# A 16-batch channel-attention block on one core: reordered loads and set-up, split products for one combined weight, and a last row stored in pieces

## What is computed

```python
g_x     = conv1x1(g_w, g_b, ctx)              # CI x N
theta_x = conv1x1(theta_w, theta_b, x)        # CI x N
phi_x   = conv1x1(phi_w, phi_b, ctx)          # CI x N
W = einsum('bnc,bcm->bnm', theta_x.T, phi_x) / N
y = einsum('bnm,bmc->bnc', W, g_x.T).T
wy = conv1x1(w_w, w_b, y)
out = bn_gamma * (wy - bn_mean) * rsqrt(bn_var + eps) + bn_beta + x
```

## Time and profile before

| | us |
|---|---|
| median of 3 runs (lowest and highest) | 789.48 (789.16 to 789.52) |
| the profiled execution, by the same clock | 790.07 |
| its span, first to last instruction | 788.3 |
| PE busy in the span | 772.0 (98%) |
| PE weight loads busy | 666.7 |
| DVE, ACT, POOL busy | 498.1, 303.7, 527.5 |

### The profile page before, as it was taken

The page is one execution under the profiler, slowest core; times in us unless marked ns, Lnnn a source line. Parts: engine busy times, 40 slices in busy tenths (PEclk is TensorE's granted clock), DMA queues, the critical chain, the costliest instruction groups (busy, mean ns, idle before and its releaser), DMA issues.

```text
span 788.3 us, 11592 instructions
## 1 busy us (share of the span) xinstructions
PE 772.0 (98%) x4045; PEld 666.7 (85%) x4045; DVE 498.1 (63%) x889; ACT 303.7 (39%) x514; POOL 527.5 (67%) x358
## 2 busy tenths in 40 slices
PE   4999999999999999999999999999999999999997
PEld 4688888888888888888888888888888888888886
DVE  3796574847657496574847657496574847657254
ACT  3634542325334243542325334243542325334131
POOL 4969785767857578585767857578585767857400
PEclk9999999999999999999999999999999999999999
DMA  9828254181733707255181733707255181730202
GB/s 237 197 108 214 107 129 192 35 226 62 178 142 74 246 0 213 106 124 195 33 228 58 178 142 72 247 0 213 106 121 198 32 228 60 178 143 1 107 1 106
DMA packets 55127, 103.17 MB, mean 131 GB/s; under 512 B 2474, under 2 KB 37956, under 8 KB 55108
## 3 DMA queue, kind: packets, MB, share of 16 engines
q1 hardware_dynamic: 52976, 101.86, 44.2%
q10 hardware_dynamic: 2132, 1.05, 0.8%
HBM read 69.35 MB, written 33.55 MB: 131 GB/s over the span
## 4 chain that ended last, share of the span: by engine, by line
PE 96%; DVE 1%; DMA 1%; ACT 1%; issue 0%; DVEq 0%; SPq 0%
PE wbank L667 57%; PE gbank L667 37%; PE wbank L830 1%; DMA ctx_sb<-in_ctx_dram 1%; PE wbank L708 1%; DVE x_sb L486 0%; PE wbank L686 0%; PE wbank L714 0%; ACT x_sb L366 0%; DVE tmp L509 0%; DVE tmp L508 0%; ACT x_hi L340 0%; DVE junk L590 0%; DVE x_sb L657 0%; DVE th_lo L583 0%
## 5 line engine op out<-in xcount | busy, mean ns | idle before, releaser
L286 POOL TENSOR_TENSOR ctxT_lo<-ctxT,ctxT_hi 128x512 fp32r<-128x512 f32 x124 | 167.2, 1349 | 205.7 <-ACT ctxT_hi L340 205.7
L297 POOL TENSOR_TENSOR ctx_sum<-ctx_sum,ctxT 128x512 f32<-128x512 f32 x108 | 157.0, 1454 | 0.2
L315 POOL TENSOR_TENSOR x_lo<-x_sb,x_hi 128x1024 fp32r<-128x1024 f32 x60 | 142.3, 2403 | 0.0
L340 ACT ACTIVATE mt<-wbank 128x512 fp32r<-128x512 f32 x64 | 37.9, 597 | 236.6 <-PE wbank L667 236.6
L657 DVE SCALAR_TENSOR_TENSOR x_sb<-wbank,const,x_sb 128x512 f32<-128x512 f32 x112 | 78.9, 747 | 73.1 <-PE wbank L667 73.1
L667 PE MATMUL wbank<-ctxT_lo,ctxT_hi 128*128 128x512 f32 x512 | 121.6, 393 | 0.0
L518 DVE TENSOR_TENSOR stage<-gbank,mt 128x384 f32<-128x384 f32 x64 | 28.3, 486 | 139.7 <-PE gbank L667 139.7
L667 PEld LDWEIGHTS wbank<-ctxT_lo,ctxT_hi 128*128 128x128 f32 x512 | 95.5, 190 | 18.7 <-POOL ctxT_lo L286 0.2
L340 ACT ACTIVATE ctxT_hi<-ctxT 128x512 fp32r<-128x512 f32 x124 | 76.5, 628 | 88.1 <-DVE ctxT L486 88.1
L667 PE MATMUL gbank<-ctxT_hi 128*128 128x384 f32 (+1 forms) x512 | 80.8, 314 | 10.1 <-ACT ctxT_hi L340 10.1
L667 PEld LDWEIGHTS gbank<-ctxT_hi 128*128 128x128 f32 x512 | 80.0, 191 | 12.0 <-issue 10.1
(11 more groups left out here) (107 smaller groups left out, 1327.4 us busy)
## 6 DMA issues: line engine op xcount, KB each, us to landing
x_sb<-in_x_dram SPq DMA_DIRECT2D x16, 2048.0 KB, 7.8
out_dram<-x_sb SPq DMA_DIRECT2D x64, 512.0 KB, 2.6
ctx_sb<-in_ctx_dram SPq DMA_DIRECT2D x60, 512.0 KB, 8.4
ctx_sb<-in_ctx_dram ACTq DMA_DIRECT2D x4, 256.0 KB, 7.1
ctx_sb<-in_ctx_dram SPq DMA_DIRECT2D x4, 256.0 KB, 7.2
x_sb<-in_L_xattn_w_w_dram SPq DMA_DIRECT2D x1, 512.0 KB, 11.7
stage<-in_L_xattn_theta_w_dram SPq DMA_DIRECT2D x1, 512.0 KB, 12.5
phi_nat<-in_L_xattn_phi_w_dram SPq DMA_DIRECT2D x1, 512.0 KB, 12.7
```

The source lines that it names most:

```text
L286: nc.gpsimd.tensor_tensor(ctxT_lo[:, c, :], turned_ctx(b, c), f(ctxT_hi[:, c, :]), ALU.subtract).then_inc(sem_, 1)
L297: nc.gpsimd.tensor_tensor(ctx_sum[:, :], ctx_sum[:, :], src, ALU.add).then_inc(ctxT_used, 1)
L315: nc.gpsimd.tensor_tensor(x_lo[:, k, :], x_sb[par][:, k, :], f(x_hi[:, k, :]), ALU.subtract).then_inc(x_lo_made, 1)
L340: nc.scalar.activation(dst, src, ACT.Copy).then_inc(sem_, 1)
```

## The change

What it does, in five parts:

1. **Loads.** `bn_var` and `bn_gamma` are loaded first, one on SP's and one on ACT's queue, into `norm_rows`. SP then loads the partition groups 0 and 1 of the first context and ACT the groups 2 and 3 (before: 0 and 2, 1 and 3), both halves ahead of the other vectors on SP. `g_w` comes right behind `w_w`, then x, then `theta_w` and `phi_w` (before: w, theta, phi, x, g).
2. **Scale.** A PE instruction of its own (`turn_norm`) turns these two vectors ahead of all else, and DVE computes the scale before its first `transpose_chunk`. The other vectors are turned behind Gram chunk 4.
3. **Z and ZB.** ACT and DVE make hi and lo parts of g_w (`g_hi`, `g_lo`), of the wide g_b (`bg_hi`, `bg_lo`) and of the turned w (`wsT_hi`, `wsT_lo`; they lie in `th_hi`, `th_lo`, `q_hi` and `q_lo`). Each fp32 matmul of `make_z` becomes three fp32r matmuls.
4. **Other work in batch 0.** `x_lo` of k = 1 moves from POOL to DVE. `next_ctx()` moves on DVE from ahead of `theta(0)` to behind the computation of `const`, and `next_hi(0)` to `next_hi(3)` move on ACT behind the parts of `t_hi`.
5. **Last row.** In the last batch, row m = 3 is made in three pieces (512, 256 and 256 positions) one after the other, each added up and stored by itself.

```diff
         first_half = x_sb[1][:, 2:4, :].rearrange("p a (b c) -> p (a b) c", b=2)
+
...
 
         FIRST_M_BANK = [wbank[4], wbank[1], wbank[2], wbank[0]]
         W_BANK = [wbank[3], wbank[4]]
+        NORM_BANK = VEC_BANK = wbank[3]
         TP_BANK = [wbank[1], wbank[2], wbank[0], wbank[3]]
...
-            load_first_ctx(sp, (0, 2), 0)
-            load_vectors(sp, range(0, 4))
-            load_first_ctx(sp, (0, 2), 1)
+            sp.dma_start(norm_rows[KC:2 * KC, :], bn_var.rearrange("(m p) -> m p", p=P)).then_inc(in_norm, 16)
+            load_first_ctx(sp, (0, 1), 0)
+            load_first_ctx(sp, (0, 1), 1)
+            load_vectors(sp, range(0, 3))
             sp.dma_start(w_nat, w_w.rearrange("(m p) c -> p m c", p=P)).then_inc(in_w1, 16)
+            sp.dma_start(g_nat, g_w.rearrange("(k p) c -> p k c", p=P)).then_inc(in_w2, 16)
+            load_x(0, 0)
             sp.dma_start(theta_nat, theta_w.rearrange("(k p) c -> p k c", p=P)).then_inc(in_w4, 16)
             sp.dma_start(phi_nat[:, :, :], phi_w.rearrange("(k p) c -> p k c", p=P)).then_inc(in_w3, 16)
-            load_x(0, 0)
-            sp.dma_start(g_nat, g_w.rearrange("(k p) c -> p k c", p=P)).then_inc(in_w2, 16)
             sp.dma_start(bp_row[:, :], phi_b.partition_broadcast(P)).then_inc(in_bp, 16)
...
-                for m in range(KC):
+                for m in range(KC if nxt else KC - 1):
                     sp.wait_ge(work_free, NO * b + NH * (m + 1))
                     sp.dma_start(out[b].rearrange("(m p) n -> m p n", p=P)[m], x_sb[par][:, m, :]).then_inc(stored, 16)
+                if not nxt:
+                    m = KC - 1
+                    for i, (a, n, bank) in enumerate(LAST_PIECES):
+                        sp.wait_ge(work_free, NO * b + (NH * m + i + 1))
+                        sp.dma_start(out[b].rearrange("(m p) n -> p m n", p=P)[:, m, a:a + n],
+                                     x_sb[par][:, m, a:a + n]).then_inc(stored, 16)
...
-            for k in range(1, KC):
+            for k in (2, 3):
...
-            load_first_ctx(act, (1, 3), 0)
-            load_vectors(act, range(4, 8))
-            load_first_ctx(act, (1, 3), 1)
+            act.dma_start(norm_rows[0:KC, :], bn_gamma.rearrange("(m p) -> m p", p=P)).then_inc(in_norm, 16)
+            load_first_ctx(act, (2, 3), 0)
             act.wait_ge(ident_done, 2)
             nc.scalar.activation(tmp[:, 7, :], ident[:, 0:KC], ACT.Sqrt)
+            load_first_ctx(act, (2, 3), 1)
+            act.wait_ge(vec_step, 1)
+            nc.scalar.activation(tmp[:, 1, :], tmp[:, 0, :], ACT.Sqrt).then_inc(root_done, 1)
+            load_vectors(act, range(3, 6))
...
+            act.wait_ge(vec_taken, 1)
             for k in range(KI):
                 nc.scalar.activation(bg_wide[:, k, :], f(ones_r[:, :]), ACT.Identity,
                                      scale=bg_col[:, k:k + 1]).then_inc(wide_made, 1)
+            act.wait_ge(in_w2, 16)
+            hi(g_hi, g_nat, g_hi_made)
+            act.wait_ge(wide_made, KI)
+            hi(bg_hi, bg_wide, bg_hi_made)
...
+                if i > 1:
+                    act.wait_ge(w_turned, i - 1)
+                    hi(wsT_hi[:, i - 2, :], W_BANK[i - 2][:, :], w_hi_made)
...
-                if first(b):
-                    next_hi(0)
-                    next_hi(1)
-                    next_hi(2)
...
-                next_hi(3)
+                if not first(b):
+                    next_hi(3)
...
                 if first(b):
-                    next_hi(4)
-                    next_hi(5)
+                    for c in range(6):
+                        next_hi(c)
...
-            dve.wait_ge(in_first[0], 16 * QT)
-            for c in range(RING):
...
+            dve.wait_ge(norm_turned, 1)
             chain(nc.vector.tensor_scalar(ve, var_, EPS, None, ALU.add))
-            dve.wait_ge(in_first[1], 16 * QT)
-            transpose_chunk(0, 4)
             dve.wait_ge(root_done, 1)
             chain(nc.vector.reciprocal(r0, root))
...
             chain(nc.vector.tensor_tensor(r0, r2, gamma_, ALU.mult))
             nc.vector.tensor_scalar(scale[:, :], r0, 1.0 / N, None, ALU.mult).then_inc(scale_made, 1)
+            for h in range(2):
+                dve.wait_ge(in_first[h], 16 * QT)
+                for c in range(RING):
+                    transpose_chunk(0, h * RING + c)
+            dve.wait_ge(vec_turned, 1)
+            nc.vector.tensor_copy(vec_cols[:, :], VEC_BANK[:, 0:3 * KC + 3 * KI]).then_inc(vec_taken, 1)
...
+            dve.wait_ge(g_hi_made, 1)
+            nc.vector.tensor_tensor(g_lo, g_nat, f(g_hi), ALU.subtract).then_inc(g_lo_made, 1)
+            dve.wait_ge(bg_hi_made, 1)
+            nc.vector.tensor_tensor(bg_lo, bg_wide, f(bg_hi), ALU.subtract).then_inc(bg_lo_made, 1)
             first_x_lo_part(0)
-            dve.wait_ge(w_turned, KI)
+            first_x_lo_part(1)
             for k in range(KI):
-                nc.vector.tensor_copy(wsT[:, k, :], W_BANK[k][:, :]).then_inc(w_taken, 1)
+                dve.wait_ge(w_hi_made, k + 1)
+                nc.vector.tensor_tensor(wsT_lo[:, k, :], W_BANK[k][:, :], f(wsT_hi[:, k, :]),
+                                        ALU.subtract).then_inc(w_taken, 1)
...
                 if first(b):
-                    next_ctx()
                     dve.wait_ge(in_bp, 16)
...
                 if first(b):
+                    dve.wait_ge(vec_taken, 1)
                     chain(nc.vector.tensor_tensor(wm, wb_, mean_, ALU.subtract))
                     chain(nc.vector.tensor_tensor(r3, wm, r0, ALU.mult))
                     chain(nc.vector.tensor_tensor(const[:, :], r3, beta_, ALU.add))
+                    next_ctx()
                     transpose_chunk(b + 1, 4)
                     transpose_chunk(b + 1, 5)
                 if nxt:
...
+                pe.wait_ge(ident_done, 2)
+                pe.wait_ge(in_norm, 16 * 2)
+                nc.tensor.transpose(NORM_BANK[:, 0:2 * KC], norm_rows, ident[0:2 * KC, 0:2 * KC]).then_inc(norm_turned, 1)
+
             def turn_vectors():
-                pe.wait_ge(ident_done, 2)
...
             def make_z():
-                pe.wait_ge(in_w2, 16)
+                pe.wait_ge(g_lo_made, 1)
                 pe.wait_ge(w_taken, 2)
                 for j in range(KC):
                     pe.wait_ge(tp_taken, (1, 2, 2, 3)[j])
+                    cols = slice(j * P, (j + 1) * P)
                     for k in range(KI):
-                        ins = nc.tensor.matmul(Z_BANK[j][:, :], g_nat[:, k, j * P:(j + 1) * P], wsT[:, k, :],
-                                               start=k == 0, stop=k == KI - 1)
+                        mm(Z_BANK[j][:, :], g_hi[:, k, cols], wsT_hi[:, k, :], k == 0, False)
+                        mm(Z_BANK[j][:, :], g_hi[:, k, cols], wsT_lo[:, k, :], False, False)
+                        ins = mm(Z_BANK[j][:, :], g_lo[:, k, cols], wsT_hi[:, k, :], False, k == KI - 1)
                     ins.then_inc(z_done, 1)
                 pe.wait_ge(tp_taken, 4)
-                pe.wait_ge(wide_made, KI)
+                pe.wait_ge(bg_lo_made, 1)
                 for k in range(KI):
-                    ins = nc.tensor.matmul(ZB_BANK[:, :], bg_wide[:, k, :], wsT[:, k, :], start=k == 0,
-                                           stop=k == KI - 1)
+                    mm(ZB_BANK[:, :], bg_hi[:, k, :], wsT_hi[:, k, :], k == 0, False)
+                    mm(ZB_BANK[:, :], bg_hi[:, k, :], wsT_lo[:, k, :], False, False)
+                    ins = mm(ZB_BANK[:, :], bg_lo[:, k, :], wsT_hi[:, k, :], False, k == KI - 1)
                 ins.then_inc(zb_done, 1)
...
-                        if c == 1:
+                        if c == RING:
                             turn_vectors()
...
+                def last_row(m):
+                    for a, n, bank in LAST_PIECES:
+                        if bank is OUT_BANK[1][0]:
+                            pe.wait_ge(work_free, NO * b + (NH + 1))
+                        for k in range(KI):
+                            q_h, q_l = q_hi[:, k, m * P:(m + 1) * P], q_lo[:, k, m * P:(m + 1) * P]
+                            mm(bank[:, 0:n], q_h, th_hi[:, k, a:a + n], k == 0, False)
+                            mm(bank[:, 0:n], q_h, th_lo[:, k, a:a + n], False, False)
+                            ins = mm(bank[:, 0:n], q_l, th_hi[:, k, a:a + n], False, k == KI - 1)
+                        ins.then_inc(out_done, 1)
```

66 lines of the change are left out of this document (40 added, 26 removed).

## The result

The changed kernel takes 795.20 us in the median of 6 executions (794.80 to 795.86), the kernel before 789.62 on the same chip (789.16 to 790.80). The ratio is 1.0067, 95% interval 1.0056 to 1.0078: slower by two thirds of a per cent. The profiled execution took 795.54 with a span of 793.8, which is 5.5 more than the span before, and its mean granted clock (TensorE's clock as a share of 2.4 GHz) is 0.995. Two executions, 859.13 us of the kernel before and 1105.55 us of the warm-start experiment, ran at mean clocks of 0.853 and 0.656 and are left out of the ratios and ranges here.

What follows compares the result with a forecast made beforehand. PE was taken as the bound (96% of the chain), with no slack to make up batch 0 delays. Stall +4.3, clock +2.4 and end -1.7 gave +5.0 on the median 789.48: 794.5 us, range 791.5 to 797.5.

Steps and rivals of the forecast that it cites:

- stall and loss of clock: Main case: PE stalls before batch 0's output rows, then runs at a lowered clock; 794.5 us, chance 0.70.
- Part 1, loads and scale: Program start: PE starts at 10.56 us, scale chain off the path, PE's 1.09 wait before w's second half gone.
- The step that the small load ahead delays the context by 0.43: Program start: a small load's issue on the queue moves PE's start from 10.13 to 10.56 us.
- Part 2, Z and ZB: Batch 0: thirty fp32r matmuls save 1.83, but Z may start later; ZB ends 0.9 earlier.
- E: End of ZB in batch 0: predicted 38.5 us, against 39.40 before.
- Part 3, the stall: Batch 0: eight turns, held by POOL through the ring, delay Q's bias term; PE stalls 6.1, output rows +4.3 us.
- Part 4, the clock: Batch 0 output rows: PE's clock falls during the stall and costs 2.4 us, between 0 and 3.1.
- Part 5, the end: Last row: shorter last DVE instruction and smaller last store give 1.7 us, bounds 0.85 to 1.9.
- Sum: Whole kernel: +4.3 + 2.4 - 1.7 = +5.0 us.
- no loss of clock: Rival: the same stall before batch 0's output rows, but full clock after; 792.1 us, chance 0.10.
- the ring that doesn't hold DVE: Rival: batch 0's eight turns pass without waiting for POOL, no stall; 786.0 us, chance 0.08.
- The worse front: Rival: late first loads or theta and phi add 1 to 3 us to the stall; 796.5 us, chance 0.12.

Runs made afterwards that it cites:

- warm-start experiment: plain Z kernel plus 15 thrown-away fp32 identity matmuls on PE while it waits for the first context; 784.56 us, ratio 0.9934.
- plain Z: Q-first kernel with Z and ZB as ten plain fp32 matmuls, without hi and lo parts of g, its bias and w; 784.80 us, ratio 0.9943.
- old-place experiment: Changed kernel with batch 1's first four context turns and their hi parts back ahead of theta(0); 788.58 us, ratio 0.9982.
- the move alone: Kernel before, with only the four turns moved behind const and their hi parts behind t_hi; 797.67 us, ratio 1.0100.
- groups experiment: Changed kernel with the first context's partition groups as before (SP 0 and 2, ACT 1 and 3); 796.9 us, one execution.
- filler: Changed kernel plus 24 thrown-away matmuls on PE in batch 0 ahead of its wait for q_lo; 794.33 us, ratio 1.0054.
- 1.17 alone: Gain at the end in the kernel before with only the last row in three pieces; 788.72 us, ratio 0.9987.
- Q-first: Changed kernel with batch 0's Q bias term, q_lo and theta(1) ahead of turns 4 to 7, likewise on ACT; 787.15 us, ratio 0.9975.
- moved `x_lo`: Q-first kernel with DVE's second x_lo moved from ahead of wsT_lo to behind the second z_lo; 784.81 us, ratio 0.9939.

## Why the prediction was right

Predicted were 794.5, a range of 791.5 to 797.5 and "slower" with 0.89; measured 795.20. The likeliest case, stall and loss of clock, is the one that came. By its steps:

**Part 1, loads and scale.** The first chunk was to come at 10.56 and came at 9.56. The step that the small load ahead delays the context by 0.43 is wrong. The issue itself was later, 1.19 and 1.33 on the two queues for 0.74, but over the twelve profiles the first turn comes no later with the changed loads (7.51 to 8.28) than with the old ones (8.11 to 8.61), and the second half comes some 2 us earlier. The scale chain was off the path, as said. PE's wait of 1.09 was replaced by one of 0.28 for ACT.

**Part 2, Z and ZB.** 6.80 were predicted for 30 matmuls, 6.87 measured. Z was to start at 30.7 to 32.3 and E to be 38.5: 31.16 and 38.03. `bg_lo` was mis-sized at 0.5 to 1.0: it took 1.51 with POOL at its sums, where `t_lo`, of the same size, takes 0.42 with POOL idle. An `x_lo` took 2.25 in place of 1.87; both stood beside POOL's sums, so the difference stays open. `g_hi` was done at 21.0, and not at 22.3 to 23.4, which made up for it. What the prediction took as a gain of 0.9 is no gain of the split products: plain Z in the new order ends at 36.19, 1.8 earlier still (1.6 earlier than the split one with the same output order). So the rest of the new front (loads, scale, `x_lo` on DVE, not taken apart) gave the whole gain, and the split, which saves 1.8 of matmuls, gave more than that back through DVE.

**Part 3, the stall.** Relative to E the steps read, predicted and measured: T ends 12.4 and 12.4; the turns start 15.9 and 15.9; POOL starts 17.5 and 17.8; DVE is free 27.4 and 27.7; the first `q_lo` is done 29.5 and 29.8; PE is ready 23.35 and 23.26. The stall of 6.1 measured 6.60. The 0.3 of POOL's start is ACT, which took the first `ctxT_hi` 0.4 after the turn (55.06), behind a gap that the trace gives no releaser for. Because E was 0.5 early and the stall 0.5 long, the output rows started at 67.89, 0.1 from the predicted 68.0. That this agrees so well is in part two errors that cancel. The old-place experiment and the move alone show the cause from both sides.

**Part 4, the clock.** 2.4 predicted, 2.53 measured, 2.91 for the move alone (82.28 - 68.52 against 10.85), 3.21 in the profile of the groups experiment (82.47 - 68.41), 0.33 with PE kept busy. The loss was rightly foreseen, but 2.4 was chosen between 0 and 3.1 and not worked out, and that it came within 0.13 is luck: the same stall costs up to 0.7 more elsewhere. The start of the program gave the upper bound. The granted clock reads 1.00 in that stretch, so that its slowness is one of the clock was argued from the durations; the warm start, with 0.83 for 1.40, bears it out.

By the rule of the Trainium skill, page "TensorE: Matmul & The Clock Gate", section "What's actually happening", an idle array is throttled and work releases it. The changed kernel agrees (0.50 in 66 to 68 after the stall, 1.00 again in 74 to 76 with PE at work), and so does the filler, with 1.00 in 62 to 66.

**Part 5, the end.** 1.7 predicted, 1.2 measured (1.17 alone). This is the term that was mis-sized. DVE's part, 0.85 net, was near (0.79 and 0.64). What was off is the landing of the small store: it was taken to give 0.85, most of the 1.02 for the missing bytes, and gave 0.44 and 0.53. A store of 128 KB needs 2.4 to land where 512 KB need 2.6, so most of it isn't transfer. The estimate from the Trainium skill, page "DMA: Bandwidth & Descriptors", section "Anatomy of one DMA — SWDGE (gpsimd) path" (a fixed cost of about 2.0 us a transfer), would have given 1.2 and was nearer than the sum, though the page states it for GpSimd's path and this was a transfer of SP's queue.

**Sum.** +4.20 (67.89 - 63.69) + 2.53 - 1.2 = +5.5, predicted +5.0; the 0.5 is the end. The rivals: no loss of clock (792.1) has fallen with the stretches, the ring that doesn't hold DVE (786.0) with the four POOL waits. The worse front (796.5) wasn't seen in the profile of the changed kernel.

**What the prediction didn't have.** The wait of 2.07 for `wsT_lo` was in its sum as a late Z, but not that in some executions the clock falls behind such a wait. It need not be long: the groups experiment has the fall behind 1.53, the old-place kernel none behind 1.53 and the changed kernel none behind 2.07. The profiles of the filler and of the groups experiment show it (0.55 and 0.60 in 30 to 34, or 0.56 and 0.59). In the old-place and Q-first kernels only the mean clocks of other executions point to it (0.995 to 0.998, and up to 4 us more, which is more than one fall of 1.48 costs). The kernel before, with its wait of 1.09 at nearly the same place, has such executions too: 9 of 49 beside the experiments show 0.997, eight of them with 790.5 to 790.9. Taking the wait away, in two different ways, narrowed the spread: 20 executions of the three kernels without it (five with the moved `x_lo`, ten of plain Z, five with the warm start) lie within 784.2 and 785.9 (one of them with a mean clock of 0.95 at the same time as the others, which nothing here explains). Why it falls in one execution and not in another stays open, and so does whether every slow execution of those kernels has its dip at that place, since only profiled ones show it.
